# Attention with 32 small heads on one core: the step's four scores in a row behind two units of maxima, and the value product whole

## The chip, the cores and the metric

One core of a Trainium2 chip runs the whole program. The time is device microseconds from the launch of the program to its end, the median over runs; lower is better. The core's engines are TensorE (matmuls and weight loads, in the order of its queue), VectorE, ScalarE, GpSimd and SyncE (which issues most of the transfers). They wait for each other by semaphores.

## The reference, cut to what matters

A layer of attention and a layer of experts, each behind a layer norm, on x of 1 x 2048 x 512, all in float32:

```
Q = (x @ Wq + bq)   # 32 heads of 16
K = (x @ Wk + bk)   # 8 key heads of 16, each shared by 4 query heads
V = (x @ Wv + bv)   # 8 value heads of 16
attn = softmax(Q K^T / sqrt(16))
x = x + (attn V) @ Wo + bo
x = x + experts(layernorm(x))   # 8 experts, the 2 best of each token
```

The change touches only softmax(Q K^T) V. Its work is 32 heads x 2048 queries x 2048 keys, with a depth of 16 in both products.

## The kernel before, in words

**Tiling.** The attention stage has N = 32 rounds: 8 key heads, and for each 4 chunks of 512 queries. A round holds REP = 4 query heads of one key head. It has NKT = 16 steps, one for each tile of 128 keys. A step makes four scores (`score_unit`, L747 to L752): each is one matmul with 128 keys as weights and 512 queries streamed, over 50 rows (three parts of 16, and two that add the shift by the row's maximum). The heads take rows 0 to 49 and 64 to 113 in turn, so two scores can run in the array side by side. ScalarE takes the exponential of each into `probs` (L591), a ring of 16 blocks that lies in `arena_p`.

**Values.** `value_product` multiplies `probs` with the values and sums over the key tiles into PSUM bank 6. Each head has 32 columns of the array, so the four heads run side by side. The operands are float32, for which the profile shows two matmul instructions each. It runs BEHIND = 2 steps behind the scores: in step kt, key tile kt - 2. Before, it is cut in two parts of 256 queries each, part 0 behind the first pair of scores and part 1 behind the second.

**Maxima.** The softmax's maxima of a later round are found beside the scores of this one. A unit (`max_unit`) is two matmuls, 128 queries against 2 x 512 keys, into two PSUM banks; VectorE reduces them to one column (L1040). The units take banks 2 and 3, and 4 and 5, in turn, and a unit waits (`m_done`) for the reduction of the unit two before it. A step has two units; `maximum_of` says which. The last 23 steps (7 of round 30, all 16 of round 31) have none, since there is no later round.

**The ring of banks.** The scores use three PSUM banks, 0, 1 and 7, in turn. `ring_bank_free` makes a score wait (`p_ready`) for the exponential of the score three before it: the fourth score of a step waits for the exponential of the first. Once a round the transposed outputs take a bank of the ring (before the scores of step 4), and once the transposed maxima do (before those of step 11). There the third score of the step waits for VectorE's normalisation (`onorm_ready`) or shift (`neg_ready`).

**The order of the work** is written out by hand in each engine's program, and TensorE's is that of `attention_step`: unit, scores 0 and 1, values part 0, unit, scores 2 and 3, values part 1. In step 3 the outputs of the round before are transposed behind that (L775), in step 10 the maxima. ScalarE runs the exponentials in order (L583 to L592). The first of a step also waits for an old value product (`pv_done`), and before the last exponential of step 1 it copies bank 6 of the round before, once the last value product of that round is done (`copy_outputs`). The value product of step 2 waits for that copy.

Of the kernel before, what the change touches and what calls it, by code (L numbers as in the profile page):

```python
# [16 lines left out]
def preln_attention_moe(nc, x, Wq, bq, Wk, bk, Wv, bv, Wo, bo, gate_w, expert_w, expert_b, out):  # L17

    _, T, D = x.shape
    E = gate_w.shape[1]  # L20
    KVD = Wk.shape[1]
    DK = 16
    G = KVD // DK
    REP = D // KVD
    KD = D // P
    CH = 512
    NC = T // CH
    TT = CH // P
    NKT = T // P
    NKC = T // CH  # L30
    N = G * NC
# [17 lines left out]
    BEHIND = 2  # L49

    SPLIT, MAX_T = 9, 10
    PRING = 16
    UNITS = NKT * REP

    SBANKS = [0, 1, 7]
# [7 lines left out]
    def maximum_of(i, kt):  # L63

        return (i + 1, AHEAD + 2 * kt) if kt < SPLIT else (i + 2, 2 * (kt - SPLIT))
# [14 lines left out]
    with ExitStack() as ctx:  # L80
        def sb(name, shape, dt=F32):
            return ctx.enter_context(nc.sbuf_tensor(name, shape, dt))

        def sem(name):
            return ctx.enter_context(nc.semaphore(name))

        bank = ctx.enter_context(nc.psum_tensor("bank", [P, 8, CH], F32))

        v_cur = sb("v_cur", [P, NKT, 2 * DK])
# [44 lines left out]
        with nc.sbuf_tensor("we_raw", [P, E, KD, D], F32) as we_raw:  # L134
# [34 lines left out]
        x2_all = sb("x2_all", [P, NKT, D])  # L169
        EA = 4  # L170
        (_, xg, xgT, lgT, _, atT_hi, atT_lo, at), (we_hi, x2T_hi, x2T_lo) = in_turn(
            [("we_hi_early", [P, EA, KD, D], F32R),
             ("xg", [P, 2, D], F32), ("xgT", [P, 2, KD, P], F32),
# [12 lines left out]
        probs = arena_p[:, :].rearrange("p (r s) -> p r s", r=PRING)  # L186
# [28 lines left out]
        p_ready = sem("p_ready")  # L215
        pv_done = sem("pv_done")
# [458 lines left out]
        def _(pe):  # L675
# [22 lines left out]
            for c in range(NC):  # L698
# [8 lines left out]
                for t in range(TT):  # L707
                    for k in range(KD):
                        mm = pe.matmul(bank[:, 5, t * KVD:(t + 1) * KVD], xT[:, c, k, t * P:(t + 1) * P],  # L709
                                       wv_sb[:, k, :], start=(k == 0), stop=(k == KD - 1))  # L710
# [15 lines left out]
            def max_unit(j, m):  # L726
                max_half(j, m, 0)
                max_half(j, m, 1).then_inc(m_full, 1)

            def max_transpose(j):  # L730
                pe.wait_ge(maxq_ready, j + 1)
                pe.transpose(bank[0:REP * TT, B_MAX, 0:P], max_q[:, :], ident[:, :]).then_inc(mT_full, 1)

            def ring_bank_free(i, entry):

                r = RING.index(entry) - len(SBANKS)
                kind, u = RING[r]
                if r < 0:
                    pe.wait_ge(p_ready, UNITS * i + u - UNITS + len(SBANKS) + 1)
                elif kind == "score":  # L740
                    pe.wait_ge(p_ready, len(SBANKS) + UNITS * i + u + 1)
                elif kind == "outputs":
                    pe.wait_ge(onorm_ready, 2 + i)
                else:
                    pe.wait_ge(neg_ready, min(i, N - 2) + 3)

            def score_unit(i, u):  # L747
                kt, h = u // REP, u % REP
                ring_bank_free(i, ("score", u))
                r = HALVES[h % 2]  # L750
                pe.matmul(bank[:, ring_bank(("score", u)), :], k_st[r:r + ROWS, i // NC % KSLOTS, kt * P:(kt + 1) * P],  # L751
                          q_st[r:r + ROWS, i % SLOTS, h, :], start=True, stop=True).then_inc(s_full, 1)  # L752

            def value_product(i, kt, part):


                if part == 0:
                    pe.wait_ge(p_ready, len(SBANKS) + UNITS * i + REP * (kt + 1))
                half = slice(part * CH // 2, (part + 1) * CH // 2)
                for h in range(REP):  # L760
                    mm = pe.matmul(bank[32 * h:32 * h + 32, 6, half], v_cur[:, kt, :],  # L761
                                   probs[:, (REP * kt + h) % PRING, half],
                                   start=(kt == 0 and part == 0), stop=(kt == NKT - 1 and part == 1),
                                   skip_group_check=True)
                if part == 1:
                    mm.then_inc(pv_done, 1)

            def output_transpose(i):
                pe.wait_ge(o_ready, i + 1)
                if i == N:  # L770
                    pe.wait_ge(p_ready, len(SBANKS) + UNITS * N)
                else:
                    ring_bank_free(i, ("outputs", 0))
                for t in range(TT):
                    mm = pe.transpose(bank[:, B_OUT, t * P:(t + 1) * P], o_acc[:, t * P:(t + 1) * P], ident[:, :])  # L775
                mm.then_inc(oT_full, 1)
# [28 lines left out]
            def attention_step(i, kt):  # L805

                j, m = maximum_of(i, kt)
                with_max = j < N
                if kt == 0:
                    pe.wait_ge(shift_dma, 1 + 64 * (i + 1))  # L810
                if kt == SPLIT and with_max:
                    pe.wait_ge(q_dma, 16 * NQD * (j + 1))
                    if j == NC:
                        pe.wait_ge(kr_dma, 16 * NKD * (KSLOTS - 1))
                    elif j % NC == 0 and j // NC >= KSLOTS:
                        pe.wait_ge(kr_dma, 16 * NKD * (j // NC))

                def values(part):
                    if kt >= BEHIND:
                        if kt == BEHIND and part == 0:  # L820
                            pe.wait_ge(v_ready, i // NC + 1)
                            pe.wait_ge(o_ready, i + 1)
                        value_product(i, kt - BEHIND, part)
                    elif i > 0:
                        value_product(i - 1, NKT + kt - BEHIND, part)

                if with_max:
                    max_unit(j, m)
                score_unit(i, REP * kt)
                score_unit(i, REP * kt + 1)  # L830
                values(0)
                if with_max:
                    max_unit(j, m + 1)
                score_unit(i, REP * kt + 2)
                score_unit(i, REP * kt + 3)
                values(1)
                if kt == BEHIND + 1:
                    output_transpose(i)
                if kt == MAX_T and i < N - 1:
                    ring_bank_free(i, ("maxima", 0))  # L840
                    max_transpose(i + 1)

            for i in range(N):
                for kt in range(NKT):
                    attention_step(i, kt)
            for kt in range(NKT - BEHIND, NKT):
                for part in range(2):
                    value_product(N - 1, kt, part)
            output_transpose(N)

            def product(out_, lhs, rhs, first=True, last=True):
# [83 lines left out]
            def halves(b):  # L935
# [4 lines left out]
                      start=True, stop=True).then_inc(tot_full, 1)  # L940
            pe.wait_ge(tot_ready, 1)
            pe.matmul(bank[:, 4, 0:P + E], before[:, :], chosen[:, :, :].rearrange("p n e -> p (n e)"),
                      start=True, stop=False)
            pe.matmul(bank[:, 4, 0:P + E], totals[:, :], before_tile[:, :, :].rearrange("p n e -> p (n e)"),
                      start=False, stop=True).then_inc(rank_full, 1)
# [353 lines left out]
```

## Time and profile before

| | |
|---|---|
| median of 2 runs | 1864.06 us (1862.76 to 1865.36) |
| the profiled execution's own time | 1858.62 us |
| its span, first to last instruction | 1857.0 us |
| mean granted TensorE clock | 0.966 |
| TensorE matmuls busy | 1692.8 us, 91% of the span |
| VectorE busy | 1449.9 us, 78% |
| ScalarE busy | 1251.2 us, 67% |
| GpSimd busy | 162.9 us, 9% |
| score matmuls (L751) | 2048, mean 411 ns |
| unit matmuls (L722) | 2048, mean 499 ns |
| value matmuls (L761) | 8192, mean 392 ns |
| reductions (L1040) | 1024, mean 1223 ns |
| exponentials (L591) | 2048, mean 596 ns |

A row's duration is from an instruction's start to its end; matmuls that run side by side or overlap have rows that overlap, so the durations of rows don't add up to time. What a step costs is read from the starts: from one group of matmuls to the next. Granted clock 1.00 is TensorE at 2.4 GHz, 0.50 at 1.2 GHz. Idle time is put down to the instruction that ended the wait.

### The profile page before, as it was taken

What the parts mean: (1) busy time and instruction counts of PE and PEld (TensorE: products, weight loads), DVE (VectorE), ACT (ScalarE), POOL (GpSimd) and SP (SyncE); (2) the same over time, 40 slices, a digit from 0 to 9 for tenths busy, and PEclk for the clock granted to TensorE, in tenths of its full rate; (3) what the DMA queues carried; (4) which work ended last, traced back from release to release, by engine and by line L of the source; (5) the groups of instructions that cost most, each with busy time, mean ns of one, the idle gap of its engine ahead of it and who ended that gap; (6) DMA issues with size and microseconds to landing.
All of it is one profiled execution on the core that took longest, in us unless ns stands there. A gap on an engine that the chain in (4) does not pass through costs nothing.

```text
span 1857.0 us, 38115 instructions
## 1 busy us (share of the span) xinstructions
PE 1692.8 (91%) x13946; PEld 814.3 (44%) x13947; DVE 1449.9 (78%) x1503; ACT 1251.2 (67%) x2291; POOL 162.9 (9%) x186
## 2 busy tenths in 40 slices
PE   6899999999999999999999999999999998569980
PEld 3533444444444444444444444444444456427860
DVE  3298999999999999999999999999999426552215
ACT  2325888888788888888888888888888863403320
POOL 3111110000000000000000000000000013070006
PEclk9998999999999999999999999999999999869995
DMA  6337332311211131113111111111120022044548
GB/s 198 83 108 162 111 110 67 70 30 22 57 29 22 22 61 22 22 22 64 34 24 44 24 22 22 44 22 22 22 44 27 5 97 69 12 170 154 167 135 256
DMA packets 76537, 125.15 MB, mean 67 GB/s; under 512 B 27976, under 2 KB 31576, under 8 KB 75648
## 3 DMA queue, kind: packets, MB, share of 16 engines
q1 hardware_dynamic: 61664, 80.38, 18.5%
q0 software_dynamic: 12304, 41.07, 6.6%
q10 hardware_dynamic: 2448, 1.84, 0.6%
q8 instruction: 106, 1.74, 0.4%
q14 instruction: 15, 0.12, 0.0%
HBM read 74.22 MB, written 47.84 MB: 66 GB/s over the span
## 4 chain that ended last, share of the span: by engine, by line
PE 82%; issue 6%; DVE 4%; POOL 3%; DMA 2%; ACT 1%; ACTq 0%; SPq 0%; DVEq 0%; POOLq 0%
PE bank L761 30%; PE bank L722 22%; PE bank L751 14%; PE bank L856 8%; PE bank L694 3%; POOL slots_x L375 1%; PE bank L775 1%; PE bank L932 1%; POOL ys L384 1%; POOL xs L384 1%; DVE o_norm L1066 1%; DVE max_kc L1040 1%; PE bank L883 1%; PE bank L709 1%; DMA arena_p<-in_L_attn_bv 1%
## 5 line engine op out<-in xcount | busy, mean ns | idle before, releaser
L1040 DVE TENSOR_REDUCE max_kc<-bank 128x1 f32<-128x1024 f32 x1024 | 1241.9, 1223 | 104.0 <-PE bank L722 84.2
L591 ACT ACTIVATE arena_p<-bank 128x512 f32<-128x512 f32 x2048 | 1108.2, 596 | 235.9 <-PE bank L751 205.0
L761 PE MATMUL bank<-arena_p,v_cur 128*32 128x256 f32 x8192 | 655.4, 392 | 3.2 <-issue 0.3
L722 PE MATMUL bank<-k_st,q_st 48*128 48x512 f32 x2048 | 513.6, 499 | 5.3 <-DMA q_st<-q_parts 4.0
L751 PE MATMUL bank<-q_st,k_st 50*128 50x512 f32 x2048 | 443.7, 411 | 33.6 <-DVE o_norm L1066 21.8
L722 PEld LDWEIGHTS bank<-k_st,q_st 48*128 48x128 f32 x2048 | 191.2, 184 | 422.4 <-issue 372.6
L751 PEld LDWEIGHTS bank<-q_st,k_st 50*128 50x128 f32 x2048 | 286.2, 185 | 80.1 <-DVE o_norm L1066 32.0
L761 PEld LDWEIGHTS bank<-arena_p,v_cur 128*32 128x32 f32 x8192 | 162.7, 108 | 292.7 <-issue 159.7
L1179 DVE TENSOR_TENSOR x2T_lo<-bank,x2T_hi 128x512 fp32r<-128x512 f32 x39 | 27.0, 691 | 103.9 <-ACT x2T_hi L597 103.9
L326 POOL COPY v_cur<-v_all 128x256 f32 (+1 forms) x8 | 3.2, 399 | 1054.7 <-PE bank L761 1054.7
L694 PE MATMUL bank<-xT,arena_p 128*128 128x512 f32 x160 | 83.7, 648 | 5.0 <-DMA arena_p<-in_L_attn_bv 2.9
L651 ACT ACTIVATE ys<-bank 128x512 f32<-128x512 f32 x39 | 23.3, 597 | 84.2 <-PE bank L856 84.2
L551 ACT ACTIVATE qf<-bank,bq_sb 128x512 f32<-128x512 f32 x16 | 11.0, 687 | 66.2 <-PE bank L694 66.2
L856 PE MATMUL bank<-we_hi,x2T_hi 128*128 x156 | 46.5, 420 | 0.1
L1064 DVE RECIPROCAL o_rec<-bank 128x16 f32<-128x16 f32 x33 | 8.2, 249 | 48.1 <-PE bank L775 48.1
L694 PEld LDWEIGHTS bank<-xT,arena_p 128*128 128x128 f32 x160 | 28.6, 199 | 35.6 <-issue 29.6
L375 POOL DMA_INDIRECT slots_x<-xn,slot_i x32 | 37.3, 1165 | 71.7 <-DVE slot_i L1222 61.1
L856 PE MATMUL bank<-we_hi,x2T_lo 128*128 x156 | 42.6, 395 | 0.0
L856 PE MATMUL bank<-we_lo,x2T_hi 128*128 x156 | 42.0, 391 | 0.0
L1268 DVE SCALAR_TENSOR_TENSOR x_all<-xs,g_w,x_all 128x512 f32<-128x512 f32 x16 | 12.1, 754 | 31.9 <-DMA ys<-slots_y,slot_i 31.9
L335 POOL TENSOR_TENSOR parts<-qf,parts 128x512 fp32r<-128x512 f32 x20 | 25.4, 1268 | 117.7 <-ACT parts L553 117.7
L608 ACT ACTIVATE xgT<-bank 128x512 f32<-128x512 f32 x16 | 9.6, 597 | 36.5 <-PE bank L873 36.5
(147 smaller groups left out, 811.5 us busy)
## 6 DMA issues: line engine op xcount, KB each, us to landing
q_st<-q_parts SPq DMA_DIRECT2D x192, 128.0 KB, 4.9
slots_x<-be_sb POOLq DMA_DIRECT2D x39, 256.0 KB, 2.3
xs<-slots_x SPq DMA_DIRECT2D x39, 256.0 KB, 2.7
slots_y<-ys SPq DMA_DIRECT2D x39, 256.0 KB, 2.0
q_parts<-parts SPq DMA_DIRECT2D x16, 512.0 KB, 3.0
we_raw<-in_L_ffn_expert_w POOLq DMA_DIRECT2D x8, 1024.0 KB, 6.4
k_st<-k_parts SPq DMA_DIRECT2D x48, 128.0 KB, 5.1
heads_out<-o_norm SPq DMA_DIRECT2D x33, 128.0 KB, 2.3
```

Source lines behind the costliest of these rows:

```text
L335: pool.tensor_tensor(parts[:, u, 1, :], qf[:, u, :], parts[:, u, 0, :].bitcast(F32), ALU.subtract).then_inc(parts_ready, 1)
L375: pool.indirect_dma_start(slots_x, bass.IndirectOffsetOnAxis(ap=slot_i[:, a, n:n + 1], axis=0), xn2[:, n % SR, :], None).then_inc(sc_dma[n ...
L384: pool.indirect_dma_start(buf[:, n % SR, :], None, slots_y, bass.IndirectOffsetOnAxis(ap=slot_i[:, a, n:n + 1], axis=0)).then_inc(yt_dma[n ...
L591: act.activation(probs[:, u % PRING, :], bank[:, ring_bank(("score", u)), :], ACT.Exp, scale=SCALE).then_inc(p_ready, 1)
L651: act.activation(ys[:, b, :], bank[:, b, :], ACT.Copy).then_inc(y_evac, 1)
L694: mm = pe.matmul(bank[:, PROJ_BANK[p], :], w, xT[:, c, k, :], start=(k == 0), stop=(k == KD - 1))
L722: return pe.matmul(bank[:, 2 + 2 * (m % 2) + q, :], q_st[r:r + CROW, j % SLOTS, h, qt * P:(qt + 1) * P], k_st[r:r + CROW, j // NC % KSLOTS ...
L751: pe.matmul(bank[:, ring_bank(("score", u)), :], k_st[r:r + ROWS, i // NC % KSLOTS, kt * P:(kt + 1) * P], q_st[r:r + ROWS, i % SLOTS, h, : ...
L761: mm = pe.matmul(bank[32 * h:32 * h + 32, 6, half], v_cur[:, kt, :], probs[:, (REP * kt + h) % PRING, half], start=(kt == 0 and part == 0) ...
L856: mm = pe.matmul(out_, a(k), w(k), start=(q == 0 and k == 0), stop=(q == 2 and k == KD - 1))
L1040: dve.reduce_max(max_kc[:, m:m + 1], bank[:, 2 + 2 * (m % 2):4 + 2 * (m % 2), :].rearrange("p a s -> p (a s)"), AX.X).then_inc(m_done, 1)
L1179: dve.tensor_tensor(x2T_lo[:, b, :, :], bank[:, 5 + b, :].rearrange("p (k s) -> p k s", k=KD), x2T_hi[:, b, :, :], ALU.subtract).then_inc( ...
```

## The change

TensorE's order in a step becomes: unit, scores 0 and 1, unit, scores 2 and 3, value product. The value product is one group of four heads over all 512 queries, in place of two groups over 256. All else stays: the ring of three banks, the two steps that the values lie behind the scores, the order on the other engines, and the amount of data.

```
-            def value_product(i, kt, part):
-                if part == 0:
-                    pe.wait_ge(p_ready, len(SBANKS) + UNITS * i + REP * (kt + 1))
-                half = slice(part * CH // 2, (part + 1) * CH // 2)
+            def value_product(i, kt):
+                pe.wait_ge(p_ready, len(SBANKS) + UNITS * i + REP * (kt + 1))
                 for h in range(REP):
-                    mm = pe.matmul(bank[32 * h:32 * h + 32, 6, half], v_cur[:, kt, :],
-                                   probs[:, (REP * kt + h) % PRING, half],
-                                   start=(kt == 0 and part == 0), stop=(kt == NKT - 1 and part == 1),
-                                   skip_group_check=True)
-                if part == 1:
-                    mm.then_inc(pv_done, 1)
+                    mm = pe.matmul(bank[32 * h:32 * h + 32, 6, :], v_cur[:, kt, :],
+                                   probs[:, (REP * kt + h) % PRING, :],
+                                   start=(kt == 0), stop=(kt == NKT - 1))
+                mm.then_inc(pv_done, 1)
...
                 if with_max:
                     max_unit(j, m)
                 score_unit(i, REP * kt)
                 score_unit(i, REP * kt + 1)
-                values(0)
                 if with_max:
                     max_unit(j, m + 1)
                 score_unit(i, REP * kt + 2)
                 score_unit(i, REP * kt + 3)
-                values(1)
+                values()
```

TensorE before, two steps in the middle of a round (L722 is a unit, L751 the scores, L761 the values; the semaphore that an instruction waits for stands in brackets):

```order
L722 MATMUL bank<-k_st,q_st 128x512 [waits m_done]
L722 MATMUL bank<-k_st,q_st 128x512
L751 MATMUL bank<-q_st,k_st 128x512 [waits p_ready] x2
L761 MATMUL bank<-arena_p,v_cur 32x256 [waits p_ready]
L761 MATMUL bank<-arena_p,v_cur 32x256 x3
L722 MATMUL bank<-k_st,q_st 128x512 [waits m_done]
L722 MATMUL bank<-k_st,q_st 128x512
L751 MATMUL bank<-q_st,k_st 128x512 [waits p_ready] x2
L761 MATMUL bank<-arena_p,v_cur 32x256 x4
```

TensorE with the change, one step at the same place (L757 is the value product's new line):

```order
L722 MATMUL bank<-k_st,q_st 128x512 [waits m_done]
L722 MATMUL bank<-k_st,q_st 128x512
L751 MATMUL bank<-q_st,k_st 128x512 [waits p_ready] x2
L722 MATMUL bank<-k_st,q_st 128x512 [waits m_done]
L722 MATMUL bank<-k_st,q_st 128x512
L751 MATMUL bank<-q_st,k_st 128x512 [waits p_ready] x2
L757 MATMUL bank<-arena_p,v_cur 32x512 [waits p_ready]
L757 MATMUL bank<-arena_p,v_cur 32x512 x3
```

Between the first and the second pair of scores there is now one unit and no value matmul; the whole value product stands behind the second pair. The step with the normalisation, TensorE with the change:

```order
L757 MATMUL bank<-arena_p,v_cur 32x512 x3
L769 MATMUL bank<-ident,o_acc 128x128 [waits p_ready,o_ready]
L769 MATMUL bank<-ident,o_acc 128x128 x3
L722 MATMUL bank<-k_st,q_st 128x512 [waits m_done]
L722 MATMUL bank<-k_st,q_st 128x512
L751 MATMUL bank<-q_st,k_st 128x512 [waits p_ready] x2
L722 MATMUL bank<-k_st,q_st 128x512 [waits m_done]
L722 MATMUL bank<-k_st,q_st 128x512
L751 MATMUL bank<-q_st,k_st 128x512 [waits onorm_ready]
L751 MATMUL bank<-q_st,k_st 128x512 [waits p_ready]
L757 MATMUL bank<-arena_p,v_cur 32x512 [waits p_ready]
```

The third score of this step waits for the normalisation as before; of the value product, the part that stood between the two pairs of scores now stands behind the wait.

## Rows read from the trace of the kernel before

**Rows 1.** The page: span, the chain that ended last, a costly group (columns there: busy, mean | idle).
```profile
span 1857.0 us, 38115 instructions
...
PE 82%; issue 6%; DVE 4%; POOL 3%; DMA 2%; ACT 1%; ACTq 0%; SPq 0%; DVEq 0%; POOLq 0%
...
L751 PE MATMUL bank<-q_st,k_st 50*128 50x512 f32 x2048 | 443.7, 411 | 33.6 <-DVE o_norm L1066 21.8 <-DVE shift L1057 11.5 <-ACT arena_p L591 0.3
```

**Rows 2.** Stretches, the attention stage: its length, each engine's busy us, granted clock.
```profile
core 0: us, PE busy (x) PEld busy (x) DVE busy (x) ACT busy (x) POOL busy (x), PEclk, DMA share, GB/s
152.08:1512.42 1360.34, 1323.40 (x12316) 575.16 (x12316) 1225.14 (x1136) 1123.40 (x2080) 33.11 (x58) 1.00 0.19 42
```

**Rows 3.** Timeline of TensorE, steps with maxima: start, duration, operation, count merged.
```profile
811.96 0.50 PE L722 MATMUL bank<-k_st,q_st 48*128 48x512 f32 x2
812.30 0.39 PE L751 MATMUL bank<-q_st,k_st 50*128 50x512 f32 x2
812.62 0.64 PE L761 MATMUL bank<-arena_p,v_cur 128*32 128x256 f32 x8
813.19 0.50 PE L722 MATMUL bank<-k_st,q_st 48*128 48x512 f32 x2
...
814.78 0.41 PE L751 MATMUL bank<-q_st,k_st 50*128 50x512 f32 x2
...
816.03 0.40 PE L751 MATMUL bank<-q_st,k_st 50*128 50x512 f32 x2
...
821.91 0.50 PE L722 MATMUL bank<-k_st,q_st 48*128 48x512 f32 x2
```

**Rows 4.** Timeline there: the exponential of a first score, the weight load of the fourth.
```profile
815.28 0.60 ACT L591 ACTIVATE arena_p<-bank 128x512 f32<-128x512 f32 x1 [0.25 <-PE bank L751]
...
815.93 0.18 PEld L751 LDWEIGHTS bank<-q_st,k_st 50*128 50x128 f32 x1
```

**Rows 5.** Timeline of TensorE and ScalarE, a step without maxima (round 31).
```profile
1490.25 0.50 PE L751 MATMUL bank<-q_st,k_st 50*128 50x512 f32 x2
...
1490.86 0.60 ACT L591 ACTIVATE arena_p<-bank 128x512 f32<-128x512 f32 x1 [0.19 <-PE bank L751]
...
1491.51 0.50 PE L751 MATMUL bank<-q_st,k_st 50*128 50x512 f32 x1
...
1491.94 0.64 PE L761 MATMUL bank<-arena_p,v_cur 128*32 128x256 f32 x8
1492.51 0.51 PE L751 MATMUL bank<-q_st,k_st 50*128 50x512 f32 x2
```

**Rows 6.** Timeline of TensorE, the last value products of the stage, in a row.
```profile
1512.42 2.37 PE L761 MATMUL bank<-arena_p,v_cur 128*32 128x256 f32 x40
```

**Rows 7.** Timeline of VectorE and ScalarE, instructions that follow each other without a gap.
```profile
820.27 4.65 DVE L1040 TENSOR_REDUCE max_kc<-bank 128x1 f32<-128x1024 f32 x4
...
823.69 1.23 DVE L1040 TENSOR_REDUCE max_kc<-bank 128x1 f32<-128x1024 f32 x1
...
1490.86 2.06 ACT L591 ACTIVATE arena_p<-bank 128x512 f32<-128x512 f32 x4 [0.19 <-PE bank L751]
```

**Rows 8.** Timeline of TensorE, start of the stage: scores, then a unit, no values yet.
```profile
152.42 0.40 PE L751 MATMUL bank<-q_st,k_st 50*128 50x512 f32 x2
152.66 0.40 PE L722 MATMUL bank<-k_st,q_st 48*128 48x512 f32 x2
```

**Rows 9.** Timeline of TensorE, step 4 of a round: its first unit, its second scores.
```profile
806.02 0.49 PE L722 MATMUL bank<-k_st,q_st 48*128 48x512 f32 x2
...
808.46 0.51 PE L751 MATMUL bank<-q_st,k_st 50*128 50x512 f32 x2 [0.71 <-DVE o_norm L1066]
```

**Rows 10.** Timeline of TensorE, step 1 of a round, where ScalarE copies the outputs.
```profile
800.55 0.40 PE L751 MATMUL bank<-q_st,k_st 50*128 50x512 f32 x2
801.04 0.64 PE L761 MATMUL bank<-arena_p,v_cur 128*32 128x256 f32 x8
```

**Rows 11.** Stretches: early steps of the stage, and steps without maxima (columns as in 2).
```profile
156.82:167.06 10.24, 10.24 (x58) 3.74 (x60) 5.83 (x6) 4.99 (x11) 1.19 (x2) 0.50 0.68 186
...
1488.00:1497.00 9.00, 9.00 (x84) 3.46 (x80) 0.77 (x1) 8.24 (x17) 0.00 (x0) 1.00 0.06 15
```

**Rows 12.** Timeline of TensorE at half clock, the units at both ends of a step.
```profile
158.09 0.79 PE L722 MATMUL bank<-k_st,q_st 48*128 48x512 f32 x2
...
162.41 0.79 PE L722 MATMUL bank<-k_st,q_st 48*128 48x512 f32 x2
```

More of the change, by code:

```diff
@@ L816, in attention_step, with values @@
                         pe.wait_ge(kr_dma, 16 * NKD * (j // NC))
-                def values(part):
+                def values():
                     if kt >= BEHIND:
-                        if kt == BEHIND and part == 0:
+                        if kt == BEHIND:
                             pe.wait_ge(v_ready, i // NC + 1)
                             pe.wait_ge(o_ready, i + 1)
-                        value_product(i, kt - BEHIND, part)
+                        value_product(i, kt - BEHIND)
                     elif i > 0:
-                        value_product(i - 1, NKT + kt - BEHIND, part)
+                        value_product(i - 1, NKT + kt - BEHIND)
                 if with_max:
@@ L846, in _ @@
             for kt in range(NKT - BEHIND, NKT):
-                for part in range(2):
-                    value_product(N - 1, kt, part)
+                value_product(N - 1, kt)
             output_transpose(N)
```

## The prediction

> **What bounds the kernel now.** I read the page first, then the stage table, then single steps of the timeline, engine by engine, since only these show which wait is close to ending last. The chain that ended last is TensorE work for 82% of the span [rows 1], and the attention stage, from 152.08 to 1512.42 us, is 1360.34 of the 1857.0 us of the span, with the clock granted at 1.00 and TensorE busy 1323.40 us of it [rows 2]. The stage is 32 rounds of 16 steps, 512 in all. Of these, 489 carry two units of maxima: 16 in each of rounds 0 to 29 and 9 in round 30. The other 23 carry scores and values alone.
>
> One step with maxima, in order: a unit's matmuls start at 811.96, the first pair of scores at 812.30, half a value product at 812.62, the next unit at 813.19 [rows 3]. Four such steps run from 811.96 to 821.91, so a step takes 2.49 us. Nothing waits long here: TensorE's own starts add up to 0.34 + 0.32 + 0.57 for a half, 2.46 for two. VectorE's reductions, fed without a gap, start 1.14 us apart ((823.69 - 820.27) / 3) [rows 7], which would allow 2.28. Four exponentials take 2.06 us in a run [rows 7]. So TensorE's order of work sets the time, with VectorE less than 10% behind.
>
> The row to look at is a wait that costs nothing yet. Call the four scores of a step s0 to s3 and their exponentials e0 to e3. Three PSUM banks serve the scores in turn, so s3 writes the bank that e0 reads, and its weight load waits for e0. In the step whose first scores start at 814.78, e0 starts at 815.28 and takes 0.60, which ends at 815.88; the weight load of s3 starts at 815.93 [rows 4]. So 0.05 us after e0, s3 is let go; the matmuls of s2 and s3 start at 816.03 [rows 3], which is when they would have come in any case. The half value product between s1 and s2 is what covers this latency.
>
> **The change part by part.** (1) Value products. 512 x 2 groups of four heads over 256 columns become 512 groups over 512 columns. A half takes 0.57 (812.62 to 813.19) [rows 3], with the switch into this mode of the array and out of it. Each head's matmul is two instructions, two passes. Ten passes in a row, 40 matmuls, take 2.37 us [rows 6]; take off the first two, which make up the 0.64 of a half [rows 3], and 1.73 is left for eight: 0.216 a pass of 256 columns. The other 256 columns add two of these, 0.43, and the whole is 1.00. Bounds: 0.86 if the switches cost nothing (four passes), 1.14 if nothing is saved (two halves). I take 1.00, as it is made of the rows of the same operation.
>
> (2) Switches between kinds of matmul. Before, every pair of scores is followed by values. Now s0, s1 are followed by a unit. The only place where a unit follows scores directly is the start of the stage: 152.42 to 152.66, 0.24 [rows 8], and the scores behind it would follow in about the same time. TensorE's own work then is 0.34 + 0.24 + 0.24 + 0.33 + 1.00 = 2.15 us a step, 0.34 less than now. If nothing else counted, this would be the gain.
>
> (3) What it costs. Between s1 and s3 there is now only one unit, 0.24 us plus the first scores' 0.24, so s3 arrives about 0.48 us after s0. It can't start then. From s0's start to e0's is 0.50 (814.78 to 815.28) [rows 3, 4], e0 takes 0.60, the release 0.05 [rows 4]: 1.15. TensorE stands still for 0.67 us less the stream of s2 in it. Behind the waiting s3 in the same queue stand the value product, whose inputs are two steps old and ready, then the next unit, and then the next s0, on which the next e0 depends. So the latency is in the loop of every step. Its length, from a unit's start to the next: 0.34 (unit to s0) [rows 3] + 0.50 + 0.60 + 0.05 + 0.43 (a score that starts alone behind this wait, to its values: 1491.51 to 1491.94) [rows 5] + 1.00 = 2.92 us. The step was 2.49: 0.43 more.
>
> This loop can be checked where it already binds, in the steps without maxima. There s0 starts at 1490.25, e0 at 1490.86 and takes 0.60, s3 starts at 1491.51, values at 1491.94, and the next s0 at 1492.51 [rows 5]: 0.61 + 0.60 + 0.05 + 0.43 + 0.57 = 2.26, just what the rows show. With the change all is the same but for the last term, 1.00 for 0.57: 2.69, again 0.43 more.
>
> (4) The other engines. ScalarE has e0 to e3 within 2.06 us and then waits for the next s0. VectorE gets its two units 0.58 us apart and has 2.92 us for 2.28 of work. Neither is late. The unit's own wait (its banks' reductions of one step before) is met: the reductions of both units end well before their turn comes. SyncE and GpSimd wait on the value products once a round or once in four; a signal that comes 0.4 us later doesn't reach TensorE, as the next use is a step away.
>
> (5) Once a round. The copy of the outputs waits for the last value product. Its delay shows before as 0.49 instead of 0.32 between scores and values (800.55 to 801.04) [rows 10], and about as much again a half step later. Now it starts later by 0.4, and the exponential behind it lets s2 of the next step go about 0.3 us late: the same cost, so nothing is added. At the normalisation, s2 waits until 808.46, 2.44 us after the unit's start at 806.02 [rows 9]. That path runs through transpose and VectorE, and is not moved; behind it stands 1.00 instead of 0.57, so this step too grows by 0.43. The same holds for the step with the shifts.
>
> (6) The first steps with values run at half clock (0.50 from 156.82 to 167.06) [rows 11], 4.32 us each (158.09 to 162.41, of two halves each 2.16) [rows 12]. There TensorE's own work hides the latency. I add nothing for four steps; two steps have no values.
>
> **Sum.** 487 + 23 - 4 = 506 steps by 0.43 = 218 us. Against the profiled execution's 1858.62 us this gives 2077 us; against the median of the runs, 1864.06, it is **2082 us**, 11.7% slower. The profiled one lies 0.3% under the median, so I give the sum on the median. With the bounds of (1), 0.29 to 0.57 a step, it would be 2011 to 2152. Half of each way covers what I doubt, for the taken value is built from rows of the same matmuls.
>
> **The rivals.** *The switches win.* If s3 were not held up (point of decision: e0 would have to be over 0.48 us after s0's start, where the rows show 1.15), VectorE would set the step: 2.28 for 2.49, 487 x 0.21 = 102 us less, 1762 us. For it: TensorE would be 0.34 us a step shorter, and it is busy nearly all the stage. Against it: s3's load stands 0.05 us behind e0 already, 1.15 us after s0. The Trainium skill, TensorEngine Tiling (Array Packing), section Key Properties, says that changing the tiling mode, and not just the tile, drains TensorE. By that rule alone the change, which halves the switches into column tiles, would be a gain; this case's rows agree that a switch costs time, but the drain is the smaller of the two terms. I give this rival 5%.
>
> *No change.* The two effects could cancel if the value product were much shorter than I think, or the order of waits other than the code says; a step of 2.49 would need a value product of 0.57 us for twice the columns, which passes of 0.216 exclude. 3%: 1864 us.
>
> *The clock falls too.* TensorE now stands still in every step, and for some 1.5 us in the two steps of a round that wait for VectorE. The trace has the clock at 0.50 for 10.24 us [rows 11] after the start of the stage, where scores waited for ScalarE and no values filled the gaps. At 4.32 us a step or more, 10.24 us hold 2.4 steps instead of 3.5, a loss of 3 us. Once a round that is 32 x 3 = 100 us, 2180 us. Against it: in the steps without maxima, 1488 to 1497, TensorE waits in each one too, and keeps 1.00 [rows 11]. 8% for this in most rounds; now and then is inside the range.
>
> **The numbers.** My forecast has 84%. The range is 2045 to 2125: half of the way to each bound, and on the upper side a few falls of the clock. Outside it lie the three rivals and the far ends of (1), together about 20%. What a measurement of this kernel can tell from no change is about 2%. Faster 0.05, same 0.03, slower 0.92.
>
> **What would show it.** In the profile after: steps of 2.92 us; s3's weight load 0.05 us after e0's end and 1.15 us after s0's start; idle time on TensorE before the score line, put down to the exponentials, of 0.2 us or more in each of some 500 steps (1.15 less 0.48 less the 0.4 or so that s2's row lasts), where now it is 0.3 us in all [rows 1]; a whole value product of 1.00 us; VectorE's reductions in pairs, and its busy share in the stage down from 90% to below 80%. I am wrong if s3 starts within 0.6 us of s0, if the value product takes under 0.86 us, or if the granted clock is not 1.00 in the middle of the stage.

## The result, and the profile after

The changed kernel takes 2235.07 us (2233.23 to 2236.90, 2 runs) against 1864.06: a ratio of 1.197, 95% interval 1.192 to 1.203. The forecast was slower, but by 11.7% with a range that ended at 2125 us. The direction was right and the size was not. One of the forecast's own signs of being wrong came true as well: the granted clock is not 1.00 in the middle of the stage.

| | before | after |
|---|---|---|
| span of the profiled execution | 1857.0 us | 2231.6 us |
| mean granted TensorE clock | 0.966 | 0.875 |
| TensorE matmuls busy | 91% | 86% |
| VectorE busy | 78% | 64% |
| ScalarE busy | 67% | 54% |
| idle before the scores' matmuls, put down to the exponentials | 0.3 us | 104.4 us |

The page of the kernel after answers to [rows 1]; its second line is the chain that ended last, the third is a group of instructions (busy, mean ns | idle before), the last the granted clock in 40 slices:

```profile
span 2231.6 us, 29923 instructions
...
PE 73%; ACT 11%; issue 7%; DVE 4%; POOL 3%; DMA 1%; ACTq 1%; SPq 0%; DVEq 0%; POOLq 0%
...
L751 PE MATMUL bank<-q_st,k_st 50*128 50x512 f32 x2048 | 701.1, 475 | 191.3 <-ACT arena_p L591 104.4
...
PEclk9999988858889988998858989978888998977995
```

ScalarE has entered the chain with 11% of the span: that is the loop of the forecast. But the last row has something that the kernel before had not. Its clock was whole through the stage, but for 10.24 us at the start [rows 11]; here slice after slice shows less than a whole clock.

One step of the kernel after at full clock, TensorE (start, duration, operation, count), answering to [rows 3]; then ScalarE and a weight load, answering to [rows 4]:

```profile
718.19 0.50 PE L722 MATMUL bank<-k_st,q_st 48*128 48x512 f32 x2
718.53 0.40 PE L751 MATMUL bank<-q_st,k_st 50*128 50x512 f32 x2
718.76 0.39 PE L722 MATMUL bank<-k_st,q_st 48*128 48x512 f32 x2
718.99 0.39 PE L751 MATMUL bank<-q_st,k_st 50*128 50x512 f32 x1
719.68 0.50 PE L751 MATMUL bank<-q_st,k_st 50*128 50x512 f32 x1 [0.30 <-ACT arena_p L591]
720.11 1.06 PE L757 MATMUL bank<-arena_p,v_cur 128*32 128x512 f32 x8
721.11 0.50 PE L722 MATMUL bank<-k_st,q_st 48*128 48x512 f32 x2
```

```profile
719.03 2.07 ACT L591 ACTIVATE arena_p<-bank 128x512 f32<-128x512 f32 x4 [0.85 <-PE bank L751]
...
719.68 0.18 PEld L751 LDWEIGHTS bank<-q_st,k_st 50*128 50x128 f32 x1 [0.73 <-ACT arena_p L591]
```

Read it as the forecast did. The first score starts at 718.53, its exponential at 719.03 (0.50), and the fourth score is let go at 719.68, 1.15 us after the first. Values follow 0.43 later, the next unit 1.00 after that. From unit to unit it is 2.92 us. Each term is the one forecast.

The stretches of the kernel after (length; busy us of TensorE, its weight loads, VectorE, ScalarE and GpSimd; granted clock, third from the end): the whole stage, answering to [rows 2], and two pieces of it:

```profile
152.00:1886.50 1734.50, 1542.88 (x8233) 579.46 (x8229) 1192.84 (x1136) 1079.40 (x2079) 33.10 (x58) 0.87 0.15 33
800.00:815.00 15.00, 12.42 (x78) 4.77 (x78) 11.92 (x12) 10.02 (x20) 1.15 (x2) 1.00 0.81 157
815.00:825.00 10.00, 10.00 (x40) 3.29 (x32) 5.07 (x5) 5.05 (x10) 0.00 (x0) 0.50 0.13 29
```

The stage grew by 1734.5 - 1360.3 = 374 us, and its mean clock is 0.87. Since the clock has two levels, 0.87 means that 2 x (1 - 0.87) = 26% of the stage, 451 us, ran at half. At 815.0 it falls. TensorE just ahead of that, and behind it:

```profile
811.84 0.50 PE L722 MATMUL bank<-k_st,q_st 48*128 48x512 f32 x2
...
812.41 0.39 PE L722 MATMUL bank<-k_st,q_st 48*128 48x512 f32 x2
814.28 0.50 PE L751 MATMUL bank<-q_st,k_st 50*128 50x512 f32 x2 [1.48 <-DVE o_norm L1058]
...
816.32 0.79 PE L722 MATMUL bank<-k_st,q_st 48*128 48x512 f32 x2
816.91 0.63 PE L751 MATMUL bank<-q_st,k_st 50*128 50x512 f32 x2
...
819.03 1.93 PE L757 MATMUL bank<-arena_p,v_cur 128*32 128x512 f32 x8
820.89 0.79 PE L722 MATMUL bank<-k_st,q_st 48*128 48x512 f32 x2
```

This is step 4 of a round. The third score waits for the normalisation until 814.28, 2.44 us after the unit, as before [rows 9]. But before, half a value product stood in that time, and the row of [rows 9] shows 0.71 us idle. Now it is 1.48 us. Behind it the clock is at half, and a step there takes 820.89 - 816.32 = 4.57 us. In step 11 the third score waits for the shift, and the pause is 1.35 us (before, 0.38):

```profile
240.52 0.50 PE L751 MATMUL bank<-q_st,k_st 50*128 50x512 f32 x2 [1.35 <-DVE shift L1049]
```

In the whole stage the trace has 43 falls of the clock: one at the start as before, one in the last round, and 41 that begin within 2 us of the end of one of these waits for VectorE. 19 of them are behind a step 4 and 22 behind a step 11. There are 61 such waits, two of them at a clock that was at half already, so some are not followed by a fall.

### The profile page after: what moved, and what is told of

Its sections match the earlier page's. It is cut to its first block, busy times and chain, and to the rows that moved or that the text cites. A ratio compares the mean times of both kernels' runs of the same rounds, so it can differ in the third digit from the quotient of the medians.

```text
span 2231.6 us, 29923 instructions
## 1 busy us (share of the span) xinstructions
PE 1908.8 (86%) x9850; PEld 815.4 (37%) x9851; DVE 1418.9 (64%) x1503; ACT 1207.9 (54%) x2291; POOL 163.6 (7%) x186
## 4 chain that ended last, share of the span: by engine, by line
PE 73%; ACT 11%; issue 7%; DVE 4%; POOL 3%; DMA 1%; ACTq 1%; SPq 0%; DVEq 0%; POOLq 0%
PE bank L757 27%; PE bank L751 21%; PE bank L722 13%; ACT arena_p L591 10%; PE bank L848 6%; PE bank L694 3%; POOL slots_x L375 1%; PE bank L769 1%; PE bank L924 1%; POOL ys L384 1%; POOL xs L384 1%; DVE max_kc L1032 1%; DVE o_norm L1058 1%; PE bank L875 1%; PE bank L709 0%
## 5 line engine op out<-in xcount | busy, mean ns | idle before, releaser
L1032 DVE TENSOR_REDUCE max_kc<-bank 128x1 f32<-128x1024 f32 x1024 | 1209.6, 1218 | 495.5 <-PE bank L722 495.4
L591 ACT ACTIVATE arena_p<-bank 128x512 f32<-128x512 f32 x2048 | 1065.0, 603 | 631.9 <-PE bank L751 631.5
L751 PE MATMUL bank<-q_st,k_st 50*128 50x512 f32 x2048 | 701.1, 475 | 191.3 <-ACT arena_p L591 104.4
L757 PE MATMUL bank<-arena_p,v_cur 128*32 128x512 f32 x4096 | 632.6, 694 | 0.0
L722 PE MATMUL bank<-k_st,q_st 48*128 48x512 f32 x2048 | 515.9, 502 | 5.4 <-DMA q_st<-q_parts 3.9
L751 PEld LDWEIGHTS bank<-q_st,k_st 50*128 50x128 f32 x2048 | 312.1, 212 | 489.6 <-ACT arena_p L591 343.8
L722 PEld LDWEIGHTS bank<-k_st,q_st 48*128 48x128 f32 x2048 | 218.3, 210 | 504.6 <-DVE max_kc L1032 268.9
L757 PEld LDWEIGHTS bank<-arena_p,v_cur 128*32 128x32 f32 x4096 | 84.9, 113 | 142.5 <-ACT arena_p L591 107.1
L581 ACT ACTIVATE o_acc<-bank 128x512 f32<-128x512 f32 x33 | 19.8, 600 | 26.9 <-PE bank L757 26.9
L924 PE MATMUL bank<-ident,xs 128*128 128x128 f32 x156 | 24.3, 280 | 10.1 <-DMA xs<-slots_x 9.8
```

The source lines that it names most:

```text
L591: act.activation(probs[:, u % PRING, :], bank[:, ring_bank(("score", u)), :], ACT.Exp, scale=SCALE).then_inc(p_ready, 1)
L722: return pe.matmul(bank[:, 2 + 2 * (m % 2) + q, :], q_st[r:r + CROW, j % SLOTS, h, qt * P:(qt + 1) * P], k_st[r:r + CROW, j // NC % KSLOTS ...
L757: mm = pe.matmul(bank[32 * h:32 * h + 32, 6, :], v_cur[:, kt, :], probs[:, (REP * kt + h) % PRING, :], start=(kt == 0), stop=(kt == NKT - 1))
L924: mm = pe.transpose(bank[:, 5 + b, k * P:(k + 1) * P], src[:, k * P:(k + 1) * P], ident[:, :])
L1032: dve.reduce_max(max_kc[:, m:m + 1], bank[:, 2 + 2 * (m % 2):4 + 2 * (m % 2), :].rearrange("p a s -> p (a s)"), AX.X).then_inc(m_done, 1)
```

## The experiments

The theory before these runs: the order costs 0.43 us a step through the ring of three banks, and the falls of the clock, another 155 us or so, come from the gap in steps 4 and 11. The rival on the clock: it falls because TensorE now stands still a little in every step. Each kernel was run beside the kernel before, which gave 1870 us (1863 to 1871) in the first group and 1866 us (1861 to 1880) in the second. A time without a range is a single run.

**Halves, but late.** The new order with the value product still cut in two.

```
                 score_unit(i, REP * kt + 1)
-                values(0)
                 if with_max:
                     max_unit(j, m + 1)
...
+                values(0)
                 values(1)
```

> The new order, but the value product still in two halves, one right behind the other. Theory (the order makes the loss, not the size of the product): the halves follow each other without a switch, four passes of 0.216 us and the way in and out as before, so the product takes 1.00 us as the whole one does, the step at full clock is 2.92 us, and the time is that of the changed kernel, 2220 to 2250 us, clock falls included. Rival (the whole product brings or costs something of its own): each half pays its switch, 1.14 us and 3.06 us a step, 2300 us; or the clock holds because there are more instructions, 2080 us.

Measured: 2224.55 us, clock in the stage 0.88. The two halves in a row, and the unit behind them:

```profile
703.75 1.07 PE L761 MATMUL bank<-arena_p,v_cur 128*32 128x256 f32 x16
704.75 0.50 PE L722 MATMUL bank<-k_st,q_st 48*128 48x512 f32 x2
```

They take 1.00 us, as the whole product does. So the size of the value product does nothing: two halves that follow each other cost what the whole one does. All of the loss comes from where it stands.

**Vector first.** The changed kernel with one move on VectorE.

```
+                        if kt == 4 and half == 0:
+                            normalise(i)
+                        if kt == MAX_T + 1 and half == 0 and not last:
+                            make_shift(i + 1, 0)
+                            make_shift(i + 1, 1)
                         if not isinstance(i, int) or j < N:
                             reduce_unit(j, m + half)
-                        if kt == 4 and half == 0:
-                            normalise(i)
...
```

> The changed kernel with one move on VectorE: in step 4 the normalisation, and in step 11 the shift, come before the reduction of that step's first unit, not behind it. TensorE's program is the same. Theory (gap): the third score of these steps no longer waits for VectorE but for the exponential like any other, so 0.95 us less in each of 62 steps, 59 us, and with the gap gone the clock stays at 1.00 in the whole stage behind its start: 2082 - 59 = 2023 us, steps of 2.92 us throughout. Rival (the small wait in each step lets the clock fall): 2235 - 59 - a little, 2150 to 2180 us, half clock for 300 us or more.

Measured: 2048.41 us (2047.28 to 2049.54; 1.097 times before, 1.090 to 1.103), 187 us less than the changed kernel. Stretches of it, rounds 0 to 30 and most of round 31 (granted clock third from the end), and a step of TensorE:

```profile
166.00:1630.00 1464.00, 1335.25 (x7981) 510.42 (x7980) 1179.88 (x1123) 1029.06 (x1994) 30.66 (x55) 1.00 0.17 36
1637.00:1695.00 58.00, 53.79 (x172) 14.34 (x171) 2.88 (x3) 28.44 (x56) 0.00 (x0) 0.50 0.01 3
```

```profile
699.56 0.50 PE L722 MATMUL bank<-k_st,q_st 48*128 48x512 f32 x2
...
701.07 0.50 PE L751 MATMUL bank<-q_st,k_st 50*128 50x512 f32 x1 [0.29 <-ACT arena_p L591]
...
702.49 0.50 PE L722 MATMUL bank<-k_st,q_st 48*128 48x512 f32 x2
```

The step is still 2.93 us, with the same wait of 0.29, and the clock is 1.00 for 1464 us. So in steps with units the small waits don't bring the clock down; the gap does. Of the miss of 25 us, some 23 are the last round: it ran at half clock for 65 us, 4.15 us a step instead of 2.69, which no theory had said. Ahead of that fall TensorE's pause was 0.53 us in nearly every step, since without units nothing stands in it:

```profile
1631.07 0.50 PE L751 MATMUL bank<-q_st,k_st 50*128 50x512 f32 x1 [0.53 <-ACT arena_p L591]
```

**The gap put into the kernel before.**

```
+                late = kt in (4, MAX_T + 1)
+                if not late:
+                    values(0)
-                values(0)
                 if with_max:
                     max_unit(j, m + 1)
                 score_unit(i, REP * kt + 2)
                 score_unit(i, REP * kt + 3)
+                if late:
+                    values(0)
                 values(1)
```

> The kernel before with one move in steps 4 and 11 of each round alone: the first half of the value product stands behind the second pair of scores, so that TensorE has nothing to do from the second unit until VectorE is done. Theory (gap): TensorE stands still for over 1.5 us there, the clock falls behind some 40 of the 62 gaps, in steps 5 and 12, by 3.4 us or more each; the wait itself costs 0.57 us a step, 35 us, and the falls 60 to 180 us: 1950 to 2080 us. Rival (the clock falls because of the small wait in every step, which this kernel doesn't have): clock 1.00 in the stage, 1890 to 1900 us.

Measured: 1974.1 us. Its whole stage, and TensorE in a step 4 and in a step 11:

```profile
153.20:1626.80 1473.60, 1389.75 (x12315) 589.79 (x12311) 1226.44 (x1136) 1123.14 (x2079) 33.10 (x58) 0.93 0.18 39
```

```profile
872.48 0.50 PE L751 MATMUL bank<-q_st,k_st 50*128 50x512 f32 x2 [1.48 <-DVE o_norm L1070]
...
942.19 0.73 PE L751 MATMUL bank<-q_st,k_st 50*128 50x512 f32 x2 [1.13 <-DVE shift L1061]
```

The same gap of 1.48 us in step 4, and one of 1.13 in step 11, in a kernel that hardly waits elsewhere, bring the clock to 0.93. There are 24 falls: the first at the start of the stage, which lasted 34 us here, 13 behind the gaps of step 4 and 10 behind those of step 11. That is 23 behind 61 gaps, fewer than the 40 that I took over from the changed kernel. With the experiment before this one, the cause is shown from both sides: taken out of the changed kernel the falls go, put into the kernel before they come.

**The value product between the pairs.**

```
                 score_unit(i, REP * kt + 1)
+                values()
                 if with_max:
                     max_unit(j, m + 1)
                 score_unit(i, REP * kt + 2)
                 score_unit(i, REP * kt + 3)
-                values()
```

> The whole value product stands between the two pairs of scores: unit, 2 scores, values, unit, 2 scores. Theory (three banks: every score waits for the exponential three before it, so a whole product can't be covered anywhere): now the second score of the next step waits for the exponential of the third of this one: 0.42 + 0.60 + 0.05 + 0.43 + 1.00 + 0.34 = 2.84 us a step at full clock, some 2040 us if the clock holds. Theory on the clock (it falls because of the gap of over 1.5 us before the third score in steps 4 and 11): that gap is filled here but for 0.5 us, so the stage stays at 1.00 and the time is 2030 to 2050. Rival on the clock (it falls because TensorE stands still 0.3 us in each step): it falls here too, 2150 to 2200 us.

Measured: 2009.05 us. The stretch of rounds 0 to 30, one of round 31, and a step:

```profile
161.00:1600.00 1439.00, 1342.83 (x8027) 511.97 (x8023) 1189.71 (x1128) 1041.27 (x2006) 31.22 (x56) 1.00 0.18 38
1605.00:1660.00 55.00, 51.45 (x168) 13.56 (x160) 2.88 (x3) 28.30 (x55) 0.00 (x0) 0.50 0.01 3
```

```profile
703.44 0.50 PE L722 MATMUL bank<-k_st,q_st 48*128 48x512 f32 x2
...
704.24 0.39 PE L751 MATMUL bank<-q_st,k_st 50*128 50x512 f32 x1
704.86 0.50 PE L751 MATMUL bank<-q_st,k_st 50*128 50x512 f32 x1 [0.23 <-ACT arena_p L591]
705.28 1.07 PE L757 MATMUL bank<-arena_p,v_cur 128*32 128x512 f32 x8
706.28 0.50 PE L722 MATMUL bank<-k_st,q_st 48*128 48x512 f32 x2
```

From 703.44 to 706.28 is 2.84 us, to the hundredth what the loop gives. Here the lone score, at 704.86, is the second of a step, and it waits for the exponential of the third of the step before. The clock holds through the rounds with units and falls in the last one, for 58 us, which was not forecast. The time is still 31 us under the forecast of 2040 and below its range. I had left out that in steps 4 and 11 the values now fill the wait for VectorE: these steps take 2.68 and 2.72 us, where the kernel before has 3.44 and 3.32.

**Both units between the pairs** (on top of vector first).

```
-                if with_max:
-                    max_unit(j, m)
                 score_unit(i, REP * kt)
                 score_unit(i, REP * kt + 1)
                 if with_max:
+                    max_unit(j, m)
                     max_unit(j, m + 1)
```

> The changed kernel with the move on VectorE (2048 us), and both units between the two pairs of scores. TensorE's work is the same. Theory (the loop is first score, exponential, fourth score, values, next first score; a unit in front of the first score is in it, one between the pairs is under the latency): 0.61 + 0.60 + 0.05 + 0.43 + 1.00 = 2.69 us a step instead of 2.92, 487 x 0.23 = 112 us less, 1936 us. Rival (TensorE's amount of work or VectorE counts, not where the unit stands): no change, 2048 us.

Measured: 1945.87 us. A step from its first scores to the next:

```profile
704.10 0.49 PE L751 MATMUL bank<-q_st,k_st 50*128 50x512 f32 x2
704.44 0.68 PE L722 MATMUL bank<-k_st,q_st 48*128 48x512 f32 x4
704.96 0.89 PE L751 MATMUL bank<-q_st,k_st 50*128 50x512 f32 x2
705.78 1.06 PE L757 MATMUL bank<-arena_p,v_cur 128*32 128x512 f32 x8
706.78 0.50 PE L751 MATMUL bank<-q_st,k_st 50*128 50x512 f32 x2
```

2.68 us for 2.69. The same work in another place is 103 us faster, though the clock was at half for the last 82 us of the stage: a unit in front of the first score is paid for, and one between the pairs is not.

**Half an exponential** (on top of vector first; half of the probabilities is left out).

```
-                    act.activation(probs[:, u % PRING, :], bank[..., :],
+                    act.activation(probs[:, u % PRING, 0:CH // 2], bank[..., 0:CH // 2],
...
-                                   probs[:, (REP * kt + h) % PRING, :],
+                                   probs[..., 0:CH // 2].unsqueeze(1).to_broadcast([P, 2, CH // 2]),
```

> The changed kernel with the move on VectorE (2048 us), but each exponential is taken of 256 of its 512 columns, and the value product streams these 256 twice, so that TensorE's work stays as it was. The other half of the probabilities is left out of the result. Theory (the exponential's whole duration stands in the loop): with d us for the shorter one, a step takes 2.92 - (0.60 - d) us; at d about 0.4 that is 2.72, and some 100 us less, 1945 us. Rival (ScalarE isn't in the loop, TensorE's queue is): 2048 us.

Measured: 1928.17 us. Its exponentials, and the units at both ends of a step:

```profile
L591 ACT ACTIVATE arena_p<-bank 128x256 f32<-128x256 f32 x2048 | 673.5, 385 | 703.6 <-PE bank L751 689.4
```

```profile
701.30 0.50 PE L722 MATMUL bank<-k_st,q_st 48*128 48x512 f32 x2
...
704.01 0.50 PE L722 MATMUL bank<-k_st,q_st 48*128 48x512 f32 x2
```

The exponential is 0.385 us instead of 0.60, and the step 2.71 instead of 2.92: the whole 0.21 shows, though ScalarE had time to spare: in the stretch shown for vector first it is busy 1029 of 1464 us. An engine that is not full can be in the loop with its latency, and not with its throughput.

**The order of before in the steps without units** (late halves in the others, and vector first).

```
+                if not with_max:
+                    values(0)
-                values(0)
                 if with_max:
                     max_unit(j, m + 1)
...
+                if with_max:
+                    values(0)
                 values(1)
```

> The changed order with the move on VectorE in the 489 steps with units (both halves of the value product behind the fourth score), and the order of before, a half behind each pair, in the 23 steps without. Theory: in the last round of the changed order the clock falls because two of five kinds of work are missing and TensorE stands still longer; with the halves between the pairs it holds as in the kernel before. 2048 less 23 x 0.43 = 10 and less some 28 for 65 us at half clock: 2010 us, clock 1.00 to the end of the stage. Rival (the last round's clock has another cause): 2038 us.

Measured: 2017.78 us, 31 less than vector first alone, and the clock holds to the end of the stage:

```profile
170.00:1670.00 1500.00, 1369.75 (x12240) 653.08 (x12239) 1182.25 (x1125) 1062.66 (x2060) 30.09 (x54) 1.00 0.16 36
```

So the order is also what brings the clock down in round 31. Ahead of that fall the rows show a pause in every step, mostly of 0.53 us in the changed kernel and of 0.45 with the values between the pairs; here and in the kernel before TensorE pauses once in the whole round, for 0.34 us. With half an exponential it was mostly 0.32 us, hardly more than the 0.29 that left the clock alone in steps with units, and the clock fell too. So the missing units seem to matter beside the pause's length; no run took the two apart.

**Vector first in the kernel before.** The same move on VectorE as above, and nothing else.

> The kernel before (halves between the pairs), with the move on VectorE alone: normalisation and shift ahead of the first reduction of steps 4 and 11. Theory: the waits of the third score there, 0.87 us in step 4 and 0.54 in step 11, go: 31 x 1.41 = 44 us, 1820 us, and since VectorE works 2.28 us of a step of 2.49 it takes up the later reduction within a step or two. It should beat both kernels. Rival: the reduction that now starts later holds up the unit two later, and the wait only moves: 1855 to 1865 us.

Measured over six runs: 1816.17 us (1810.07 to 1822.23), 0.973 times before, interval 0.971 to 0.976. The idle time of TensorE and its weight loads before the scores, by what ended it (us, times), in the kernel before and in this one:

```profile
  DVE o_norm L1066: 53.8, 63
  DVE shift L1057: 32.4, 60
```

```profile
  issue: 11.5, 28
  ACT arena_p L591: 8.9, 25
  DVE o_norm L1066: 0.4, 1
```

The two waits of VectorE are gone, and nothing takes their place; the time is the 1820 us of the forecast within 4. This is faster than both kernels by 2.7% and 18.7%.

## Why the prediction was wrong

**The loop was right, term by term.** Part (3) gave 2.92 us a step; the trace has 2.92. Moving the values, moving the units and shortening the exponential changed the step to 2.84, 2.68 and 2.71, where the loop gives 2.84, 2.69 and 2.71. The value product of part (1) is 1.00, whole or in late halves. The total of 218 us fits too: of the 374 us by which the stage grew, 441 us at half clock (451 less the 10 that were there before) cost 441 x (1 - 2.92 / 4.57) = 159, and 215 are left.

**What failed is the term for falls of the clock, which the sum put at nothing.** The forecast named it as a rival with 8% and 100 us; it happened and cost about 159 us (the 155 of the experiments' theory). I had the gap of 1.5 us in the two steps of a round in hand, as part (5) puts the whole value product behind the wait. The step that failed is the argument against the rival: that the clock stayed at 1.00 from 1488 to 1497 though TensorE waits in each of those steps. TensorE's rows show no idle time there at all, 9.00 us busy of 9.00 [rows 11]: half a value product and the third score cover the wait for the exponential. I judged a pause of 1.5 us by steps that hold none. The runs show that pauses of 0.29 us leave the clock alone in steps with units (1464 us at 1.00), and that one pause of 1.35 or 1.48 us among them can bring it down. No row of the kernel before could have shown it, since its longest pause in the rounds is 0.71 us [rows 9]. The start of the stage, which I named, is no such row either: the clock falls there behind steps without values, and their only pause is 0.31 us:

```profile
153.60 0.50 PE L751 MATMUL bank<-q_st,k_st 50*128 50x512 f32 x1 [0.31 <-ACT arena_p L591]
```

**The size** of the rival was off in the number of falls. I took one a round, 32; there were two places a round, and 41 falls. Their mean length was 10.3 us, near the 10.24 that I had taken, which is luck: most lasted one to three steps, and five lasted 31 or 55 us. The price of a step at half clock was low as well. Part (6) has TensorE's own work hide the latency there and takes 4.32 us; in the changed kernel the fourth score's weight load waits 0.63 us for the exponential at half clock too, and the step is 4.57:

```profile
817.66 2.07 ACT L591 ACTIVATE arena_p<-bank 128x512 f32<-128x512 f32 x4 [1.76 <-PE bank L751]
...
818.30 0.28 PEld L751 LDWEIGHTS bank<-q_st,k_st 50*128 50x128 f32 x1 [0.63 <-ACT arena_p L591]
```

**Part (5) was right and incomplete.** The step with the normalisation grew by 0.43, as said. What I did not ask is what the half value product did for TensorE while it stood in that wait: it kept the pause at 0.71 us [rows 9].

**The rival that the switches win** had its term right: TensorE's starts up to the wait are 0.34, 0.23 and 0.23 apart. It was not reached, since the latency decides. Where the Trainium skill, TensorEngine Tiling (Array Packing), section Key Properties, has the array drain at a change of mode, the late halves agree: four passes in a row, with one way in and out, took 1.00 us, where two separate halves take 1.14.

## What to carry to other kernels

Where a ring of few buffers makes a producer wait for a reader, write down the loop of latencies through the in-order queue; work that stands between a buffer's filling and its reuse is free up to that latency, and the same work behind the wait is paid in full. Before moving work out of a wait, look at how long the engine will stand still there, and not only at what the wait costs: here one pause of 1.1 to 1.5 us of TensorE could put the steps behind it at half clock. On the other engines, put the short operations that the busiest engine waits for ahead of the long ones that it doesn't.

## What the runs showed of the hardware

The clock can fall behind a single pause of 1.1 to 1.5 us in a stretch where TensorE is otherwise busy. It did so behind 41 of 61 such pauses in the changed kernel (mostly 1.48 us in step 4, 1.35 in step 11) and behind 23 of 61 in the kernel before with the gap put in (1.48 and 1.13). Pauses of 0.71 us there never did it in 30 rounds, and 0.29 us in every step with units did not either. In steps without units pauses of 0.32 to 0.53 us in nearly every step were followed by a fall. Whether a pause leads to a fall differs from round to round, and why was not tested. The Trainium skill, TensorE: Matmul & The Clock Gate, section Why this matters for your kernels, warns only of pauses longer than these; here the measurement decides.

A step of mixed small matmuls took 4.57 us at half clock and 2.92 at full, 1.57 times and not twice. ScalarE does not slow down (four exponentials in a run take 2.07 us at either level): the exponential and its release are 0.60 and 0.04 us at half clock too. TensorE's own terms of the loop, 0.34 + 0.50 + 0.43 + 1.00 = 2.27 us, became 0.59 + 0.75 + 0.73 + 1.86 = 3.93, that is 1.73 times, just as the kernel before's whole step did (2.49 to 4.32).
